# ScalarE takes the last sequence's last values and gates ahead of the first sequence's second normalisation

## The chip, the core and the metric

The kernel runs on one NeuronCore of a Trainium2 chip. The time is device microseconds of one launch, from the first to the last work of the core; the median of several runs is compared. A profiled execution of the kernel gives the span (first to last instruction) and the trace.

## What is computed

A decoder layer for four sequences of 1024 tokens with 256 features, in three stages, each followed by a layer normalisation of input plus result:

```python
# stage 1: gated convolution and a linear recurrence
proj = einsum('btd,ed->bte', x, W_in)          # gate and value halves
g = sigmoid(gate); v = conv5(val) + conv_b     # depthwise, 5 taps
h = tanh(a_param) * h + g * v                  # scan over the tokens
y1 = layernorm(x + einsum('btd,ed->bte', h, W_out)) * ln_w + ln_b
x = layernorm(x + y1)                          # "second normalisation"
# stage 2: three iterations of attention from 1024 slots on 64 context rows, each with a GRU cell
x = layernorm(x + slots)
# stage 3: every token goes to the expert (of 8) with the highest score
x = layernorm(x + (x + expert(x)))
```

## The kernel before

The first stage runs sequence by sequence (b = 0 to 3), in two chunks of 128 features (c = 0, 1), all within the first 170 us. Each engine has one hand-written list of steps, which it works through strictly in the order of the code; semaphores tie the lists together. What happens around the change:

- TensorE, `project(b)` (line 1152) makes the values and gates in PSUM, two banks each; `output(b)` (line 1167) multiplies the scanned result by W_out, in two halves of four token tiles; `transposes(b)` (line 1188) turns the normalised rows feature-major; `low_parts(b)` (line 1197) subtract the rounded part from what was turned. Its list reads: `project(3, 1, C)`, `transposes(0)`, `output(2, 0, TJ)`, `low_parts(0)`, `output(2, TJ, NT)`, `transposes(1)`, `spread(0)`, `low_parts(1)`, `first_scores(0)` (line 1267).
- ScalarE, `values(b, c)` (lines 551 to 569) copies the values out of PSUM, makes the first convolution tap with its bias, and the gates with a sigmoid; `window(w)` (line 571) loads the table with logarithm and exponential and makes reciprocal standard deviations; `first_rows` and `second_rows(b)` (lines 584 and 590) apply a normalisation to eight tiles of rows; `new_slots(b)` (line 651) copies the turned rows out of PSUM, twice; `row_roots` (line 596) and `low_slots` (line 662) follow.
- VectorE, `taps` (line 1632) makes the other four convolution taps, `scan` (line 1650) the recurrence, `residual(b)` (line 1661) adds `output(b)` to x in four pairs of tiles and takes the statistics, `second(b)` (lines 1703 to 1713) prepares the second normalisation, `offsets(w)` (lines 1680 to 1688) follows `window(w)`, and `first_tops` (line 1729) reads the first scores.
- GpSimd makes one product of gates and convolution per sequence (line 983) and adds a bias (line 976).

Three waits matter here. `transposes(0)` waits for all sixteen gate copies, which the last step of `values(3, 1)` completes, for the low value parts, and per tile for `n2_done`, which `second_rows(0)` counts up. `residual(2)` comes behind `offsets(2)` on VectorE, and the second half of `output(2)` needs a PSUM bank that the first pair of `residual(2)` frees. `rss[:, 1]`, which `second_rows(0)` reads as its scale, is written again by `window(2)`.

Of the kernel before, what the change touches and what calls it, by code (L numbers as in the profile page):

```python
# [27 lines left out]
def decoder_layer(nc, x, xT, ctxT, vecs, w_inT, w_outT, wq, wkT, wvT, wihT, whhT, gateT, expertT,  # L28
# [7 lines left out]
    NT = T // P  # L36
# [36 lines left out]
    with root:  # L73
# [5 lines left out]
        def sem(name):  # L79
            return root.enter_context(nc.semaphore(name))  # L80
# [27 lines left out]
        def col(c, i):  # L108
            return vec[:, c, i:i + 1]
# [37 lines left out]
        n1_done, n2_done = sem("n1_done"), sem("n2_done")  # L147
# [261 lines left out]
        def value_bank(i):  # L409
            return TBS[i % 2]  # L410

        def high_part(i):
            return 4 * (i // 2) + i % 2
# [4 lines left out]
        def cols_of(j):  # L418
            return slice(j * BANK, (j + 1) * BANK)
# [4 lines left out]
        with nc.Block(no_gpsimd_drain=True) as block:  # L424
# [125 lines left out]
            def _(act):  # L550
                def values(b, c):
                    n = C * b + c
                    if b > 0:
                        act.wait_ge(conv, TAPS * (n - C + 1))
                    for j in range(J):
                        act.wait_ge(val_mm, J * n + j + 1)
                        act.activation(val[:, c, HALO + j * BANK:HALO + (j + 1) * BANK],
                                       psum[:, VB + j, :], ACT.Copy).then_inc(val_ev, 1)
                    act.wait_ge(val_ev, J * n + J)
                    if b > 1:  # L560
                        act.wait_ge(scanned, n - 2 * C + 1)
                    act.activation(cvs[b % 2][:, c, :], val[:, c, 0:T], ACT.Identity, bias=col(c, V_CB),
                                   scale=col(c, 0)).then_inc(tap_act, 1)
                    if b > 1:
                        act.wait_ge(out_mm, NT * (b - 1))
                    for j in range(J):
                        act.wait_ge(gate_mm, J * n + j + 1)
                        act.activation(gates[:, b % 2, c, cols_of(j)], psum[:, GB + j, :],
                                       ACT.Sigmoid).then_inc(gate_ev, 1)

                def window(w):

                    lo, hi, n1, n2 = WINDOWS[w]
                    if w in (1, 2, 6):
                        act.preload_act_table_set("natural_log_exp_and_others")
                    if n1 > 0:
                        act.wait_ge(agg1, NT * n1)
                    if n2 > 0:
                        act.wait_ge(agg2, NT * n2)
                    act.activation(rss[:, lo:hi], mvs[:, lo:hi, :, 1], ACT.Ln, bias=epsc[:, 2:3]).then_inc(ln_act, 1)  # L580
                    act.wait_ge(ln_act, 2 * w + 1)
                    act.activation(rss[:, lo:hi], rss[:, lo:hi], ACT.Exp, scale=-0.5).then_inc(ln_act, 1)
# [7 lines left out]
                def second_rows(b, lo=0, hi=NT):  # L590
                    act.wait_ge(off2, b + 1)
                    for t in range(lo, hi):
                        act.activation(res[:, b % 2, t, :], res[:, b % 2, t, :], ACT.Identity,
                                       bias=nms[:, 1, t:t + 1], scale=rss[:, 1, t:t + 1]).then_inc(n2_done, 1)
# [40 lines left out]
                def free_part(n):  # L635
                    if n > 2:
                        act.wait_ge(vp_out[n % 3], 64 * (n // 3))
# [7 lines left out]
                def value_low(i):  # L645
                    act.wait_ge(vp_sub, i + 1)
                    free_part(high_part(i) + 2)
                    act.activation(value_parts[(high_part(i) + 2) % 3][:], psum[:, value_bank(i), 0:HG],
                                   ACT.Copy).then_inc(vp_lo, 1)
# [62 lines left out]
                values(3, 0)  # L712
                value_low(2)
                value_low(3)
                second_rows(0)
                values(3, 1)
                window(2)
                new_slots(0)
                row_roots(1)
# [1654 lines left out]
```

## Time and profile before

| what | value |
|---|---|
| median of 3 runs | 556.05 us (555.78 to 556.29) |
| profiled execution | 555.52 us |
| its span | 553.7 us |
| mean granted clock of TensorE | 0.963 |
| busy in the span: TensorE, VectorE, ScalarE, GpSimd | 91%, 79%, 61%, 45% |

The profiled execution's time is 1.8 us longer than its span, for what lies around the first and the last instruction. In the rows below PE is TensorE, PEld its weight loads, DVE is VectorE, ACT ScalarE and POOL GpSimd. "128x512 f32<-128x512 f32" is the shape written and read. Matmuls are pipelined, so one started while another still runs.

### The profile page before, as it was taken

How to read it: one execution, taken by the hardware profiler on the slowest of the kernel's cores; microseconds unless marked ns; L12 is line 12 of the kernel's file. 1: busy time of each engine (PE TensorE's matmuls, PEld its weight loads, DVE VectorE, ACT ScalarE, POOL GpSimd, SP SyncE). 2: the span in 40 equal slices, each digit the busy share in tenths (PEclk: the TensorE clock that was granted, in tenths of full speed). 3: DMA queues.
4: the chain of work that ended last, by engine and by line, in shares of the span. 5: the costliest groups of instructions: out<-in, count | busy, mean ns of one | idle time of the engine just before them, and what ended most of it. 6: DMA issues, size and time to landing. Idle time of an engine off the chain costs nothing.

```text
span 553.7 us, 7262 instructions
## 1 busy us (share of the span) xinstructions
PE 504.1 (91%) x2154; PEld 363.6 (66%) x2154; DVE 440.0 (79%) x794; ACT 340.5 (61%) x600; POOL 251.7 (45%) x217
## 2 busy tenths in 40 slices
PE   6999986959779999899999999999997999979992
PEld 2465552725557687488768867885885788767771
DVE  2999999998799487989967985897677567868882
ACT  4557539784697574667466656765663766557452
POOL 0123050400223256556835664575335156737776
PEclk9999999879889999999999999999997999989997
DMA  8950435420021031000000000002111136255742
GB/s 286 336 189 2 124 67 140 125 78 1 0 77 72 6 78 77 0 2 0 2 0 1 0 0 1 1 2 76 40 38 38 39 126 237 87 163 161 235 138 71
DMA packets 30661, 43.13 MB, mean 78 GB/s; under 512 B 7933, under 2 KB 22398, under 8 KB 30336
## 3 DMA queue, kind: packets, MB, share of 16 engines
q1 hardware_dynamic: 27216, 34.25, 20.5%
q0 software_dynamic: 3408, 8.43, 4.2%
q8 instruction: 18, 0.29, 0.2%
q14 instruction: 19, 0.16, 0.1%
HBM read 25.70 MB, written 16.83 MB: 77 GB/s over the span
## 4 chain that ended last, share of the span: by engine, by line
PE 51%; issue 6%; DVE 6%; POOL 4%; ACT 3%; DMA 1%; SPq 0%; POOLq 0%; ACTq 0%; DVEq 0%
PE psum L1456 35%; PE psum L1549 7%; PE psum L1267 3%; PE psum L1398 2%; PE psum L1520 2%; PE psum L1344 1%; POOL gru L1019 1%; DVE gru L1872 1%; POOL out L1057 1%; POOL sorted_rows L1049 1%; DVE slots_full L1874 1%; POOL slots_lo L1034 1%; PE psum L1356 1%; DVE gru L1852 1%; PE psum L1420 1%
## 5 line engine op out<-in xcount | busy, mean ns | idle before, releaser
L1456 PE MATMUL psum<-slots_hi,w_hh 128*128 128x512 f32 x560 | 181.5, 406 | 1.2 <-ACT gru L766 1.2
L1456 PEld LDWEIGHTS psum<-slots_hi,w_hh 128*128 128x128 f32 x560 | 104.5, 191 | 27.9 <-issue 4.2
L1019 POOL TENSOR_TENSOR gru<-slots_full,gru 128x512 f32<-128x512 f32 x43 | 65.9, 1531 | 111.6 <-ACT gru L772 111.6
L1456 PE MATMUL psum<-slots_lo,w_hh 128*128 128x512 f32 x280 | 112.3, 401 | 0.0
L1456 PE MATMUL psum<-at,v_ih_pair 128*128 128x512 f32 x288 | 92.6, 406 | 4.6 <-DVE at L1751 3.1
L772 ACT ACTIVATE gru<-gru,vec 128x512 f32<-128x512 f32 x48 | 34.7, 722 | 59.1 <-DVE gru L1852 59.0
L1456 PEld LDWEIGHTS psum<-at,v_ih_pair 128*128 128x128 f32 x288 | 54.6, 193 | 21.6 <-DVE at L1751 3.4
L1845 DVE SCALAR_TENSOR_TENSOR gru<-psum,vec,gru 128x512 f32<-128x512 f32 x48 | 35.9, 748 | 35.6 <-PE psum L1456 29.8
L1152 PE MATMUL psum<-early_hi,w_in 128*128 128x512 f32 x128 | 57.3, 606 | 5.2 <-DMA early_hi<-in_xT 5.1
L1456 PEld LDWEIGHTS psum<-slots_lo,w_hh 128*128 128x128 f32 x280 | 53.4, 191 | 12.9
L1872 DVE TENSOR_TENSOR gru<-gru 128x512 f32<-128x512 f32 x47 | 43.7, 930 | 7.2 <-POOL gru L1019 3.7
L1152 PEld LDWEIGHTS psum<-early_hi,w_in 128*128 128x128 f32 x128 | 24.6, 195 | 35.5 <-issue 33.9
L1034 POOL TENSOR_TENSOR slots_lo<-slots_full,slots_hi 128x512 fp32r<-128x512 f32 x32 | 47.1, 1473 | 0.6 <-DVE slots_hi L1898 0.6
L766 ACT ACTIVATE gru<-psum,brz 128x512 f32<-128x512 f32 x48 | 32.7, 681 | 21.4 <-PE psum L1456 21.3
L1874 DVE TENSOR_TENSOR slots_full<-gru 128x512 f32<-128x512 f32 x47 | 44.5, 947 | 1.6
L1549 PE MATMUL psum<-slots_full,w_tile 128*128 x156 | 43.5, 401 | 0.4 <-issue 0.2
L1057 POOL DMA_INDIRECT out<-out_tile,out_index x39 | 38.0, 975 | 11.9 <-issue 8.5
L1049 POOL DMA_INDIRECT sorted_rows<-row_block,dest x32 | 33.8, 1056 | 19.9 <-DVE dest L1960 8.5
L1028 POOL TENSOR_TENSOR ss_block<-sq_block 128x512 f32<-128x512 f32 x16 | 22.3, 1396 | 40.3 <-ACT sq_block L787 36.8
L1852 DVE TENSOR_TENSOR gru<-psum,gru 128x512 f32<-128x512 f32 x48 | 33.2, 691 | 6.7 <-PE psum L1456 5.0
L779 ACT ACTIVATE gru<-psum,brz 128x512 f32<-128x512 f32 x48 | 32.6, 678 | 0.9 <-PE psum L1456 0.6
L1167 PE MATMUL psum<-w_out,gates 128*128 128x256 f32 x128 | 29.2, 382 | 4.2 <-DVE res L1661 3.5
(249 smaller groups left out, 868.1 us busy)
## 6 DMA issues: line engine op xcount, KB each, us to landing
gathered<-sorted_rows SPq DMA_DIRECT2D x39, 129.0 KB, 2.4
x_scratch<-slots_full SPq DMA_DIRECT2D x8, 512.0 KB, 3.0
x_block<-x_scratch SPq DMA_DIRECT2D x8, 512.0 KB, 4.3
early_hi<-in_xT SPq DMA_DIRECT2D x3, 1024.0 KB, 5.7
v_ih_pair<-value_part SPq DMA_DIRECT2D x32, 96.0 KB, 2.2
x_tm<-in_x SPq DMA_DIRECT2D x4, 512.0 KB, 7.0
slots_full<-expert_plus SPq DMA_DIRECT2D x1, 2048.0 KB, 10.1
sorted_rows<-gru SPq DMA_DIRECT2D x1, 1032.0 KB, 11.4
```

Of the source, the lines that this page charges most:

```text
L772: act.activation(X(u), X(u), ACT.Tanh, bias=col(c, V_BIH + 2)).then_inc(n_act, 1)
L1019: pool.tensor_tensor(DF(u), full[:, c, seq(k, h), blk(j)], X(u), ALU.subtract).then_inc(d_pool, 1)
L1034: last = pool.tensor_tensor(slots[1][:, c, b, blk(j)], full[:, c, b, blk(j)], slots[0][:, c, b, blk(j)].bitcast(F32), ALU.subtract)
L1049: pool.indirect_dma_start(rows[:], bass.IndirectOffsetOnAxis(dest[:, n:n + 1], 0), rowb[:, row_slot(n), :], None, bounds_check=E * REGION - 1,
L1057: pool.indirect_dma_start(out[:], bass.IndirectOffsetOnAxis(oidx[:, g % 4, t:t + 1], 0), og[:, i % (4 * TG), :], None, bounds_check=TOK - ...
L1152: last = pe.matmul(psum[:, bank + j, :], wi[:, k, at_col:at_col + P], xF[b % 2][:, k, cols_of(j)], start=k == 0, stop=k == C - 1)
L1456: last = pe.matmul(psum[:, bank, :], w, d, start=start and i == 0, stop=stop and i == len(pairs) - 1, skip_group_check=begun or late)
L1549: last = pe.matmul(expert_out(i), wT[:, i % TG, c, :], ew[:, c, bass.ds(off, D)], start=c == 0, stop=c == C - 1)
L1845: dve.scalar_tensor_tensor(out=X(u), in0=psum[:, hn_bank(u), :], scalar=col(c, V_BHH + 2), in1=X(u), op0=ALU.add, op1=ALU.mult).then_inc(t ...
L1852: dve.tensor_tensor(X(u), psum[:, XN_B, :], X(u), ALU.add).then_inc(t2_dve, 1)
L1872: dve.tensor_tensor(Z(u), Z(u), DF(u), ALU.mult).then_inc(e_dve, 1)
L1874: dve.tensor_tensor(full[:, c, seq(k, h), blk(j)], X(u), Z(u), ALU.add).then_inc(s_dve, 1)
```

## The change

ScalarE's list had `second_rows(0)` and then `values(3, 1)` behind the low value parts. Now `values(3, 1)` comes first. Since `second_rows(0)` then stands directly ahead of `window(2)`, which overwrites the scales that it reads, ScalarE waits between the two until all eight rows have been finished (`n2_done` at NT = 8).

```diff
                 values(3, 0)
                 value_low(2)
                 value_low(3)
+                values(3, 1)
                 second_rows(0)
-                values(3, 1)
+                act.wait_ge(n2_done, NT)
                 window(2)
                 new_slots(0)
                 row_roots(1)
```

No other engine's list is changed, and no instruction but the wait is added.

## Rows read from the trace of the kernel before

**Rows 1.** The page: busy us (share of the span) and instructions of each engine.

```profile
PE 504.1 (91%) x2154; PEld 363.6 (66%) x2154; DVE 440.0 (79%) x794; ACT 340.5 (61%) x600; POOL 251.7 (45%) x217
```

**Rows 2.** Timeline of ScalarE: start us, us, line, operation, tiles, count [idle before].

```profile
89.58 4.04 ACT L593 ACTIVATE res<-res,nms,rss 128x256 f32<-128x256 f32 x8
93.52 1.07 ACT L557 ACTIVATE early_lo<-psum 128x512 f32<-128x512 f32 x2
...
95.77 1.06 ACT L568 ACTIVATE gates<-psum 128x512 f32<-128x512 f32 x2
96.85 1.28 ACT L575 ACT_TABLE_LOAD   x1
...
98.59 0.58 ACT L659 ACTIVATE slots_full<-psum 128x512 f32<-128x512 f32 x1
...
101.93 0.66 ACT L660 ACTIVATE slots_hi<-psum 128x512 fp32r<-128x512 f32 x1
105.37 0.30 ACT L599 ACTIVATE rrs<-rrs,epsc 128x8 f32<-128x8 f32 x1 [2.78 <-DVE rrs L1688]
```

**Rows 3.** Timeline of TensorE, the last projection.

```profile
84.94 7.28 PE L1152 MATMUL psum<-early_hi,w_in 128*128 128x512 f32 x16
```

**Rows 4.** Timeline of TensorE, behind the last projection to the last transposes.

```profile
96.88 3.47 PE L1188 MATMUL psum<-ident,res 128*128 128x128 f32 x16 [4.66 <-ACT gates L568]
100.19 3.62 PE L1167 MATMUL psum<-w_out,gates 128*128 128x256 f32 x16
103.46 1.29 PE L1197 MATMUL psum<-slots_hi,neg 128*128 128x512 f32 x4
106.08 3.69 PE L1167 MATMUL psum<-w_out,gates 128*128 128x256 f32 x16 [1.33 <-DVE res L1661]
...
123.18 5.70 PE L1267 MATMUL psum<-slots_full,fold 128*64 128x512 f32 x16 [1.19 <-ACT slots_lo L667]
...
148.62 1.22 PE L1456 MATMUL psum<-at,v_ih_pair 128*128 128x512 f32 x2 [3.13 <-DVE at L1751]
...
162.76 0.73 PE L1456 MATMUL psum<-at,v_ih_pair 128*128 128x512 f32 x2 [1.42 <-DVE gru L1852]
165.03 2.17 PE L1188 MATMUL psum<-ident,res 128*128 128x128 f32 x8 [1.54 <-ACT res L593]
```

**Rows 5.** Timeline of VectorE, from the last taps to the first scores.

```profile
97.37 5.43 DVE L1632 SCALAR_TENSOR_TENSOR slots_full<-early_lo,vec,slots_full 128x1024 f32<-128x1024 f32 x4
...
102.99 2.35 DVE L1688 TENSOR_TENSOR rrs<-rrs,rss 128x8 f32<-128x8 f32 x1
105.25 0.68 DVE L1661 TENSOR_TENSOR res<-psum,x_tm 128x512 f32<-128x512 f32 x1
...
109.81 0.69 DVE L1661 TENSOR_TENSOR res<-psum,x_tm 128x512 f32<-128x512 f32 x1 [0.25 <-PE psum L1167]
...
129.02 1.23 DVE L1729 CUSTOM_DVE_ANT_0 sc<-psum,inv 128x1024 f32<-128x1024 f32 x1 [0.77 <-PE psum L1267]
```

**Rows 6.** Stretches: length, each engine's busy time (count), granted clock, DMA share, GB/s.

```profile
96.00:98.00 2.00, 1.12 (x5) 1.12 (x6) 2.00 (x2) 1.98 (x3) 0.00 (x0) 0.65 1.10 314
100.00:102.00 2.00, 2.00 (x12) 1.79 (x11) 1.79 (x3) 2.00 (x6) 0.00 (x0) 0.99 0.28 108
...
104.00:106.00 2.00, 0.75 (x4) 0.27 (x2) 1.97 (x3) 0.60 (x3) 1.31 (x1) 1.00 0.36 133
...
148.00:152.00 4.00, 3.38 (x8) 2.74 (x9) 3.04 (x4) 3.43 (x8) 0.00 (x0) 0.50 0.00 0
...
164.00:168.00 4.00, 2.97 (x11) 2.17 (x12) 3.87 (x5) 4.00 (x9) 2.38 (x6) 0.61 0.00 0
```

**Rows 7.** The chain that ended last, in order of time: start us, us, what.

```profile
228.49 3.65 PE psum L1267 x16
...
424.12 1.25 PE psum L1398 x4
...
427.89 0.47 PE psum L1398 x4
```

## The prediction

> **What bounds the kernel now.** I read the page first. TensorE is busy for 91% of the span and VectorE for 79% [rows 1]. A share over the whole span says nothing of one stage, so I went to the stretch that the diff touches, 84 to 130 us, one engine at a time, and asked of each engine where it stood idle and for whom.
>
> ScalarE runs without a gap from the eight rows of `second_rows(0)` (89.58) through `values(3, 1)` (93.52 to 96.83), the table load (96.85) and `window(2)` to the last piece of `new_slots(0)` (101.93 to 102.59). Then it stands for 2.78 us, until VectorE has written `rrs` [rows 2]. So ScalarE's finish in this stage has slack.
>
> TensorE ends `project(3, 1, C)` at 84.94 + 7.28 = 92.22 [rows 3] and stands 4.66 us for the gates of `values(3, 1)`, because `transposes(0)` waits for the last gate. Then come the transposes (96.88), the first half of `output(2)` (100.19), the low parts (103.46 to 104.75), another 1.33 us of waiting for VectorE's residual sum, and the second half of `output(2)` (106.08 to 109.77) [rows 4].
>
> VectorE is the one that doesn't stop: four convolution taps from 97.37, then `offsets(2)`, whose last instruction takes 2.35 us beside GpSimd's product of the same time, then the four residual pairs. Its only wait is 0.25 us ahead of the fourth pair, for the second half of `output(2)` [rows 5]. Both other engines meet VectorE here, ScalarE at 105.37 and TensorE at 106.08. VectorE sets the time, with TensorE's second half of `output(2)` 0.25 us behind it.
>
> **The change, part by part.** It adds no work but one wait, and moves two blocks past each other. *The block of ScalarE.* `values(3, 1)` took 96.83 - 93.52 = 3.31 us; put at 89.58 it ends at 92.89. Its inputs are there: its last gate half would start some 2.7 us into the block, about 92.3, and the matmul that feeds it ends at 92.22 [rows 2, 3]. The margin is under 0.1 us, so this wait costs nothing to 0.1 us. The eight rows take 4.04 us and overlap their neighbour by 0.1, so they end at about 96.8, where the old order ended. The table load starts there as before; no load is added, because the rows use a function that needed none at 89.58 either. The sum on ScalarE is 3.31 + 4.04 either way.
>
> *The added wait* (`n2_done` for all eight rows) stands behind the last row. The load of before starts 0.02 us after the end of the preceding instruction anyway, so I take 0 and bound it by 0.1 us, the overlap that back-to-back activations show. Queued behind it are the load, `window(2)`, `new_slots(0)` and `row_roots(1)`; those who want them are VectorE's `offsets(2)`, which stands behind the taps that end at 102.80 and so comes 4 us after the `window(2)` of before, and TensorE's low parts. The 2.78 us of idle time hide all of it. If that cover were gone, it would cost its 0.1 us.
>
> *Who gets what earlier or later.* The first convolution tap comes 3.9 us earlier, and VectorE wants it only behind `residual(2)`, whose fourth pair starts at 109.81 [rows 5]. The rows of `second_rows(0)` come 3.2 us later, and only the transposes read them. `transposes(0)` can now follow the rows one by one, from about 93.4 to 97.3 rather than 96.88 to 100.35. `new_slots(0)` found its transposes ready at 98.59 before, and is held by ScalarE's own order, so it gains nothing. The first half of `output(2)` starts when VectorE's scan ends, about 97.4 by the taps behind it [rows 5], rather than at 100.19, and ends near 101.1. VectorE reads it first at 105.25, so this gains nothing either. The DMA queue issues what it issued, at the same events. Some 3 us of TensorE's time are freed, but all of them are freed ahead of a rendezvous at 106.08 that VectorE sets. The gain is 0.
>
> *The price to look for* is TensorE's clock. The wait of 4.66 us goes. In its place, after the first half of `output(2)` ends near 101.1, there are only four low parts, tied to the pieces of `new_slots(0)` (the last ready at 102.6), and then nothing from about 103.0 to 106.08: 3.0 us idle where there were 1.33. The trace shows what gaps do. It fell to half, 1.2 GHz, in the gap of 4.66 us, at about 96.6 (0.65 over 96 to 98), ahead of 148.62 after 3.13 us idle (0.50 over 148 to 152), and ahead of 165.03, where 0.73 us of matmul stood between gaps of 1.42 and 1.54 us. It did not fall in the 1.33 us ahead of 106.08 [rows 4, 6]. The new gap with its sparse forerun is nearest to that of 148.62, so I hold a fall near 106 to 107 for likelier than not, 7 in 10. Its cost: the first cold stretch lasted from 96.6 to 100.0, 3.4 us (0.99 over 100 to 102) [rows 6]. Half the matmuls of a warm stretch of that length are lost, so the second half of `output(2)` ends some 1.7 us later (3.69 us for 16 warm; all cold, 7.4 us, is the upper end, 3.7 us more). VectorE's fourth pair already waits, so that passes straight on to the statistics, to `window(3)` and to `first_rows(2)`.
>
> From there it can grow or shrink. It grows to about 2.5 us if the first scores, 5.70 us in the trace for 16 matmuls that take 3.65 when warm [rows 4, 7], then run wholly cold (7.3 us, 1.6 more, less the 0.8 us that VectorE waits for them at 129.02 [rows 5]). It shrinks where a later cold stretch on the chain moves or goes: that of 164 to 168 (0.61, so 3.1 of 4 us at half [rows 6]) holds the last transposes and costs about 1.6 us now, and the chain at 424.12 shows 1.25 us for four matmuls that take 0.47 at 427.89 [rows 7]. So the cost of a fall, carried to the end, lies between -1 and +2.5 us.
>
> A rule of the Trainium skill ("TensorE: Matmul & The Clock Gate", Part 1) is that the array drops to half rate after being idle long enough and warms again only after sustained work, and that the monitor runs free of the kernel's own start, so that the place of the drop can vary between runs. By that rule the fall is to be feared here. The trace agrees with both levels; the runs of before, within 0.5 us of each other, don't show the variation.
>
> **The rivals.** *A, forecast: no change that can be measured.* Either the clock doesn't fall in the new gap (3 in 10; the gap is split by four low parts, or the late transposes still bring the old fall and the first half of `output(2)` runs cold and fills the gap), or it falls and later stretches give most of it back. For it: every edge that the change moves ends at VectorE's queue. Change 0 to +0.7 us. Sum: 555.52 (the profiled execution) + 0.1 = 555.62; the median of the runs lies 0.53 above that execution, so 556.15.
>
> *B, slower: the clock falls ahead of the second half of `output(2)`* and the 1.7 to 2.5 us stay. It decides from the point where TensorE ends those 16 matmuls more than 0.25 us after VectorE wants them, and is over the bound from 1.1 us on. Against it: the two give-backs. Time 557.7 to 558.6.
>
> *C, faster.* Either a shifted cold stretch at 165 or 421 is lost by the shift and nothing is paid for it, which is worth 1.6 us less what the first fall cost, or the freed 3 us reach someone whom I hold to be covered. Time about 554.5 to 554.9. *D: the change does not do what it says*, because the last gate half waits for TensorE: then `transposes(0)` starts up to 0.1 us later. It ends in A, as the 2.78 us hide it.
>
> **How the numbers follow.** A measurement of this kernel can tell about 0.2%, 1.1 us, from no change. A (with D) 0.55, B 0.33, C 0.12. The forecast is A's 556.15. The range reaches from inside C, 554.8, to B's end, 558.6; outside are about half of C and a little of B. Faster 0.12, same 0.55, slower 0.33.
>
> **What would show it.** In the changed profile: `values(3, 1)` at about 89.6 and the rows of `second_rows(0)` at 92.8 with no gap; transposes from 93.4 at the pace of the rows; the table load at 96.8 to 96.95; TensorE idle from about 103 to 106.1; ScalarE idle again ahead of `rrs` at 105.37. The granted clock from 106 to 110 decides between A and B: if it is full, the fourth residual pair starts at 109.8; if it is at half, at about 111.4. Wrong would be a residual pair that starts before 105.25, or a ScalarE that reaches 102.6 much later.

## The result

The changed kernel took 557.68 us in the median of 6 runs (557.37 to 559.64), beside 555.91 us for the kernel before in the median of 6 (554.89 to 557.00): 1.77 us more, a ratio of 1.004 with a 95% interval of 1.0023 to 1.0056. By the ratio the change makes this kernel slower by 0.4%, and the interval does not contain 1. The profiled execution took 559.64 us, the slowest of its six, with a span of 557.8 us. So the trace shows the loss larger than the median does: its span is 4.1 us longer than that of before, where the medians differ by 1.77.

The page of the changed kernel, busy time, and the granted clock in 40 slices:

```profile
PE 506.5 (91%) x2154; PEld 362.9 (65%) x2154; DVE 439.4 (79%) x794; ACT 340.6 (61%) x600; POOL 251.4 (45%) x217
...
PEclk9999999777998999999999999999998999989997
```

Instruction counts are those of [rows 1], and VectorE and ScalarE are busy for as long as before within 0.6 us. What was added is not work. TensorE's 2.4 us more of busy time is the same matmuls taking longer. Over the whole span its mean granted clock is no lower than before (0.964 and 0.963), so the average hides the cause: what counts is which matmuls run in the cold stretches (those at half clock).

**ScalarE, where the change was made.** The changed kernel's timeline of ScalarE:

```profile
89.85 1.12 ACT L557 ACTIVATE early_lo<-psum 128x512 f32<-128x512 f32 x2
...
92.14 1.06 ACT L568 ACTIVATE gates<-psum 128x512 f32<-128x512 f32 x2
93.10 4.04 ACT L593 ACTIVATE res<-res,nms,rss 128x256 f32<-128x256 f32 x8
97.16 1.28 ACT L575 ACT_TABLE_LOAD   x1
...
102.25 0.66 ACT L660 ACTIVATE slots_hi<-psum 128x512 fp32r<-128x512 f32 x1
105.61 0.30 ACT L599 ACTIVATE rrs<-rrs,epsc 128x8 f32<-128x8 f32 x1 [2.71 <-DVE rrs L1689]
```

This execution was 0.26 us later than that of before from well ahead of the change (its last projection starts at 85.20, that of [rows 3] at 84.94). Taken off, the last piece of `new_slots(0)` starts at 101.99, where it stood at 101.93 in [rows 2]. The swap and the added wait together cost ScalarE 0.06 us, and the idle time behind hides it: 2.71 us where there were 2.78. The side that was edited loses nothing.

**TensorE, where the loss is.** Its timeline in the changed kernel (compare [rows 4]):

```profile
93.84 3.79 PE L1189 MATMUL psum<-ident,res 128*128 128x128 f32 x16 [1.36 <-ACT res L593]
97.79 3.72 PE L1168 MATMUL psum<-w_out,gates 128*128 128x256 f32 x16 [0.16 <-DVE gates L1651]
101.16 1.31 PE L1198 MATMUL psum<-slots_hi,neg 128*128 128x512 f32 x3
102.95 0.49 PE L1198 MATMUL psum<-slots_hi,neg 128*128 128x512 f32 x1 [0.48 <-ACT slots_hi L660]
106.33 6.27 PE L1168 MATMUL psum<-w_out,gates 128*128 128x256 f32 x16 [2.88 <-DVE res L1662]
...
126.01 6.62 PE L1268 MATMUL psum<-slots_full,fold 128*64 128x512 f32 x16 [1.19 <-ACT slots_lo L667]
```

The transposes follow the rows from 93.84 and the first half of `output(2)` starts as soon as VectorE's scan is done, so the 4.66 us of idle time are gone. But the second half still starts when VectorE frees its bank, at 106.33. The idle time has moved there: 2.88 us where there were 1.33. Then the same 16 matmuls take 6.27 us instead of 3.69. The stretches of the changed kernel say why (length, busy time of the five engines, granted clock, DMA share, GB/s; compare [rows 6]):

```profile
96.00:98.00 2.00, 1.68 (x9) 0.82 (x8) 2.00 (x2) 1.98 (x4) 0.00 (x0) 1.00 1.09 324
...
102.00:104.00 2.00, 0.97 (x2) 0.35 (x2) 1.97 (x4) 0.90 (x2) 0.78 (x1) 1.00 0.75 284
104.00:106.00 2.00, 0.00 (x0) 0.00 (x0) 2.00 (x2) 0.35 (x2) 1.56 (x1) 0.68 0.51 193
106.00:108.00 2.00, 1.67 (x4) 1.43 (x5) 1.93 (x6) 2.00 (x6) 1.63 (x2) 0.50 0.00 0
...
110.00:112.00 2.00, 2.00 (x8) 1.60 (x6) 1.45 (x3) 2.00 (x5) 1.11 (x1) 0.61 0.00 0
```

The granted clock fell to half (1.2 GHz) in the new gap, at about 104.7, and came back between 110 and 112. The half clock lasted 6.8 us. In the kernel before it fell at about 96.6 and was full again from 100 on, after 3.4 us. The cold stretch has moved from work that nobody waited for (the transposes) to work that VectorE waits for, as VectorE's timeline shows:

```profile
105.50 0.68 DVE L1662 TENSOR_TENSOR res<-psum,x_tm 128x512 f32<-128x512 f32 x1
...
110.11 0.69 DVE L1662 TENSOR_TENSOR res<-psum,x_tm 128x512 f32<-128x512 f32 x1 [1.77 <-PE psum L1168]
...
112.63 0.69 DVE L1662 TENSOR_TENSOR res<-psum,x_tm 128x512 f32<-128x512 f32 x1 [1.04 <-PE psum L1168]
...
132.78 1.23 DVE L1730 CUSTOM_DVE_ANT_0 sc<-psum,inv 128x1024 f32<-128x1024 f32 x1 [1.70 <-PE psum L1268]
```

VectorE now waits 1.77 + 1.04 us where it waited 0.25 [rows 5], so the fourth pair is late by 112.63 - 109.81 - 0.26 = 2.56 us, which is the sum of the waits less the 0.25. At the first scores the delay is 132.78 - 129.02 - 0.26 = 3.50 us, because those ran cold almost to their end: they took 0.92 us more (6.62 us for 5.70), and VectorE's wait for them grew by 0.93 (1.70 for 0.77). After that it changes little: the scores of the first full round of units start at 232.65 in the chain of waits against 228.49 in [rows 7], 3.9 us later with the offset taken off, and the spans differ by 4.1 us.

### The profile page after: what moved, and what is told of

Its sections match the earlier page's. It is cut to its first block, busy times and chain, and to the rows that moved or that the text cites. A ratio compares the mean times of both kernels' runs of the same rounds, so it can differ in the third digit from the quotient of the medians.

```text
span 557.8 us, 7262 instructions
## 1 busy us (share of the span) xinstructions
PE 506.5 (91%) x2154; PEld 362.9 (65%) x2154; DVE 439.4 (79%) x794; ACT 340.6 (61%) x600; POOL 251.4 (45%) x217
## 4 chain that ended last, share of the span: by engine, by line
PE 51%; issue 6%; DVE 6%; POOL 4%; ACT 3%; DMA 1%; SPq 0%; POOLq 0%; ACTq 0%; DVEq 0%
PE psum L1457 35%; PE psum L1550 7%; PE psum L1268 3%; PE psum L1399 2%; PE psum L1521 2%; PE psum L1345 1%; POOL gru L1020 1%; DVE gru L1873 1%; POOL sorted_rows L1050 1%; POOL out L1058 1%; DVE slots_full L1875 1%; POOL slots_lo L1035 1%; PE psum L1357 1%; PE psum L1421 1%; DVE gru L1853 1%
## 5 line engine op out<-in xcount | busy, mean ns | idle before, releaser
L1457 PE MATMUL psum<-at,v_ih_pair 128*128 128x512 f32 x288 | 91.1, 400 | 5.1 <-DVE at L1752 3.1
L1168 PE MATMUL psum<-w_out,gates 128*128 128x256 f32 x128 | 31.8, 407 | 5.3 <-DVE res L1662 4.5
```

The source lines that it names most:

```text
L1457: last = pe.matmul(psum[:, bank, :], w, d, start=start and i == 0, stop=stop and i == len(pairs) - 1, skip_group_check=begun or late)
```

## Experiments

The two theories: *the clock* (the moved idle time lets TensorE's clock fall just ahead of matmuls that VectorE waits for), and *ScalarE's side* (the new order or its added wait costs the time in a way that the profile hides). In each session the kernel before ran on the same chip; its median was 555.90, 555.95 and 556.82 us.

**The changed kernel again.**

> The changed kernel again, for a yardstick on this chip beside the others. Both theories: 1.3 to 2.5 us above the kernel before, about 557.7. In the profile the second half of output(2) (16 matmuls behind the gap of 2.9 us) takes 5 to 6.5 us at half clock, where the kernel before took 3.69.

558.07 us (557.12 to 558.75, 7 runs) against 555.90 (554.61 to 557.92, 30 runs), ratio 1.0041 (1.0024 to 1.0059). TensorE's timeline in its trace, and two stretches of it:

```profile
98.10 4.15 PE L1168 MATMUL psum<-w_out,gates 128*128 128x256 f32 x16
...
106.64 6.67 PE L1168 MATMUL psum<-w_out,gates 128*128 128x256 f32 x16 [2.87 <-DVE res L1662]
```

```profile
94.00:96.00 2.00, 1.73 (x8) 0.88 (x8) 1.97 (x3) 2.00 (x6) 0.00 (x0) 0.90 0.98 321
...
104.00:106.00 2.00, 0.00 (x0) 0.00 (x0) 2.00 (x2) 0.07 (x1) 1.87 (x1) 0.96 0.68 255
```

The time is as expected, and the trace is a second sample of the mechanism; the 6.67 us lie just above the 5 to 6.5 expected. The clock fell twice here, at about 95.6 and, after it had been full again from 99, at about 105.8. So the earlier fall didn't prevent the second one: the first half of `output(2)` ran partly cold (4.15 us for 3.72), and a gap of 2.87 us was still left.

**Fill the gap.** The change stays as it is; TensorE gets work to do in the gap.

```diff
+                def keep_busy(n, bank=2):
+
+                    for _ in range(n):
+                        pe.matmul(psum[:, bank, 0:D], ident[:], wo[:, 0, :], start=True, stop=True)
+
...
                 low_parts(0)
+                keep_busy(6)
                 output(2, TJ, NT)
```

> The changed kernel with six extra f32 matmuls (twelve instructions as traced, 2.7 us at full clock) on TensorE between low_parts(0) and the second half of output(2), into a bank that nobody reads; their result is not used. Clock theory: the gap shrinks from 2.9 to about 0.2 us, the granted clock stays full from 104 to 112, the second half of output(2) takes 3.7 us again, VectorE's fourth pair waits 0.2 to 0.3 us, and the time is back within 0.5 us of the kernel before. Rival theory (ScalarE's new order or its added wait costs the time, and the clock is a bystander): the time stays 1.3 to 2.5 us above the kernel before, or more by the extra work.

556.00 us (12 runs), ratio to the kernel before 1.0007 (0.9995 to 1.0019). The median lies 0.1 us above that of the kernel before, so the loss is gone, with more work on the engine than either kernel has. TensorE's timeline and, in the last line, VectorE's fourth pair:

```profile
104.09 2.75 PE L1305 MATMUL psum<-w_out,ident 128*128 128x256 f32 x12
107.13 3.69 PE L1168 MATMUL psum<-w_out,gates 128*128 128x256 f32 x16 [0.29 <-DVE res L1668]
```

```profile
110.86 0.69 DVE L1668 TENSOR_TENSOR res<-psum,x_tm 128x512 f32<-128x512 f32 x1 [0.25 <-PE psum L1168]
```

The second half is back at 3.69 us and VectorE's wait at 0.25, to the digit those of before. ScalarE's order and its wait are those of the change. The rival theory expected 1.3 us or more; the interval ends at 0.19%, 1.1 us.

**Fill a third of the gap.** As above with `keep_busy(2)`.

> As the last, with two extra matmuls (0.9 us at full clock), so that about 2.0 us of the gap stay. Clock theory: somewhere between; a gap of 2.1 us ahead of a residual step at 71 us left the clock full in the kernel before, so I expect no fall in most executions and a time 0 to 1.2 us above the kernel before. Rival theory: 1.3 to 2.5 us above.

556.29 us (554.97 to 558.81, 12 runs), ratio 1.0008 (0.9991 to 1.0025). In the median it lies in the expected band, but in the profiled execution (558.31 us) the clock fell in the gap of 2.0 us:

```profile
106.83 5.19 PE L1168 MATMUL psum<-w_out,gates 128*128 128x256 f32 x16 [2.01 <-DVE res L1668]
```

with a granted clock of 0.61 over 106 to 108. The gap of 2.12 us at 71 us in the kernel before, where the clock stayed full, was no safe bound. Two of the twelve runs (558.31 and 558.81) lie above all 30 of the kernel before (up to 557.92), and seven lie at 556.33 or below. I read it as falling in some executions and not in others; one trace doesn't show that, nor in how many.

**Hold the transposes back.** ScalarE keeps the new order, TensorE gets its old block back.

```diff
                         pe.wait_ge(fold_ev, C)
                         pe.wait_ge(vp_lo, B)
+                        pe.wait_ge(n2_done, NT)
```

> The changed kernel with one more wait on TensorE: transposes(0) starts only when all eight rows of second_rows(0) are done. ScalarE keeps the new order and its added wait, and TensorE gets back the block of before (transposes from about 97.2, first half of output(2) to about 104, low parts to about 105, gap ahead of the second half about 1.2 us). Clock theory: time within 0.3 us of the kernel before. Rival theory (ScalarE's side): 1.3 to 2.5 us above it.

555.93 us (12 runs), ratio 1.0012 (0.9997 to 1.0026). TensorE's timeline:

```profile
97.70 3.65 PE L1190 MATMUL psum<-ident,res 128*128 128x128 f32 x16 [4.90 <-ACT res L593]
101.14 4.36 PE L1168 MATMUL psum<-w_out,gates 128*128 128x256 f32 x16
105.15 1.28 PE L1199 MATMUL psum<-slots_hi,neg 128*128 128x512 f32 x4
106.66 3.69 PE L1168 MATMUL psum<-w_out,gates 128*128 128x256 f32 x16 [0.23 <-DVE res L1663]
```

Making TensorE wait longer takes the loss away: the median is that of the kernel before within 0.03 us. The block is late and partly cold (4.36 us for the first half), but it is not waited for, and it closes the gap in front of the half that is, to 0.23 us, where I had expected about 1.2. By the interval a cost of up to 0.26% (1.4 us) for ScalarE's side can't be excluded from these runs alone; those of the full filling leave 1.1, and in the traces ScalarE was late by 0.06 us and nobody waited for it.

**The gap without the change.** The kernel before, with ScalarE untouched, and the first half of `output(2)` cut down to one matmul of 64 columns per tile instead of two of 256. This leaves out part of the output projection for four tiles of the third sequence.

```diff
+                        if b == 2 and t < TJ:
+                            last = pe.matmul(psum[:, OB + q % 2, (t % 2) * D:(t % 2) * D + 64],
+                                             gates[:, b % 2, 0, t * P:(t + 1) * P], wo[:, 0, 0:64],
+                                             start=True, stop=True)
+                            last.then_inc(out_mm, 1)
+                            continue
```

> The kernel before, ScalarE's order untouched, but the first half of output(2) shrunk to eight traced matmul instructions of 64 columns (of the four tiles' 16 of 256), so that its result is cut short there; it ends near 101.2 instead of 103.8. The gap ahead of the second half of output(2) then is about 3.0 us as in the changed kernel. Clock theory: the granted clock falls in that gap in most executions, the second half takes 5 to 6.5 us, and the time is 1 to 2 us above the kernel before although there is less work. Rival theory (ScalarE's side of the change costs the time): no change, 555.9.

558.08 us (557.39 to 560.01, 6 runs) against 555.95 (24 runs), ratio 1.0051 (1.0032 to 1.0071). TensorE:

```profile
99.61 1.64 PE L1167 MATMUL psum<-w_out,gates 128*128 128x64 f32 x8
101.06 1.01 PE L1203 MATMUL psum<-slots_hi,neg 128*128 128x512 f32 x3
102.55 0.50 PE L1203 MATMUL psum<-slots_hi,neg 128*128 128x512 f32 x1 [0.48 <-ACT slots_hi L660]
105.96 6.26 PE L1173 MATMUL psum<-w_out,gates 128*128 128x256 f32 x16 [2.92 <-DVE res L1667]
```

VectorE's third and fourth pairs:

```profile
109.75 0.69 DVE L1667 TENSOR_TENSOR res<-psum,x_tm 128x512 f32<-128x512 f32 x1 [1.77 <-PE psum L1173]
...
112.27 0.69 DVE L1667 TENSOR_TENSOR res<-psum,x_tm 128x512 f32<-128x512 f32 x1 [1.04 <-PE psum L1173]
```

Less work for TensorE, and 2.1 us more by the medians, as with the change. The gap of 2.92 us is near the changed kernel's 2.88, the duration behind it is 6.26 us for 6.27, and VectorE's two waits are the same to the digit. The clock theory is shown from both sides: filling the gap takes the loss away, and opening it without the change brings it.

**What other cold stretches cost.** The prediction had counted on later cold stretches moving or going. Three kernels take them away from the kernel before by small matmuls of `ident` on itself into an idle bank, at the places named in the expectations, for example:

```diff
                 spread(0, OB)
+                keep_busy(16)
                 low_parts(1)
```

> The kernel before with extra small matmuls on TensorE (results unused, an idle bank) in the gap of 4.1 us ahead of low_parts(1) and between those. Clock theory: the first scores run warm, 3.7 us instead of 5.0 to 6.6, VectorE no longer waits for them (0.8 us in the trace of before), time 0.5 to 1 us below the kernel before. Rival theory (the extra matmuls get in the way): 0 to 1 us above.

554.97 us (12 runs), ratio 0.9983 (0.9967 to 0.9999). As expected. The first scores and VectorE's reading of them:

```profile
123.42 3.65 PE L1269 MATMUL psum<-slots_full,fold 128*64 128x512 f32 x16 [0.59 <-ACT slots_lo L667]
```

```profile
128.46 1.23 DVE L1738 CUSTOM_DVE_ANT_0 sc<-psum,inv 128x1024 f32<-128x1024 f32 x1
```

They are warm (at full clock), 3.65 us, and VectorE no longer waits for them. The interval ends just below 1.

> The kernel before with extra small matmuls only in the two gaps of 1.4 and 1.5 us ahead of the last transposes (about 161.3 to 165.0). Clock theory: the last transposes and the unit behind them run warm; where the clock fell there, which it does in some executions only, 1.6 us are saved, so 0.3 to 1.6 us below the kernel before in the median. Rival theory: no change, as another engine has slack to give, or up to 0.5 us above.

554.52 us (12 runs), ratio 0.9983 (0.9968 to 0.9997). The last transposes run at full clock:

```profile
164.00:168.00 4.00, 3.63 (x24) 2.60 (x24) 3.87 (x5) 4.00 (x8) 2.40 (x6) 1.00 0.00 0
```

where [rows 6] had 0.61 over the same stretch. By the ratio it is worth about 0.9 us, by the medians 1.4, both in the expected band.

> The kernel before with the fillers of the last two, and also in the gaps of 2.3 and 0.7 us ahead of the token tiles at 417 to 424 and in the gap of 2.4 us ahead of the first gathered tile at 487. Clock theory: no cold stretch between 104 and the last tiles; 0.8 + 1.6 + 1.7 + 1.6 us if each were cold in every execution, 1.5 to 4 us below the kernel before in the median, and a narrower spread of its runs than the 3.3 us of before. Rival theory: no change or up to 1 us above.

553.39 us (552.15 to 555.27, 7 runs), ratio 0.9959 (0.9941 to 0.9978): 2.6 us by the medians. The spread of its runs is 3.1 us, no narrower than the 3.0 us of the 24 runs beside it, so that part of the expectation was wrong. So was the one of no cold stretch behind 104: in its trace they stood at 134 to 138 and 151 to 155, where nothing had been filled.

**Both together.** Does the time that the change frees on TensorE become worth something once the clock is looked after?

> The changed kernel with all the fillers of the earlier run on the kernel before (ahead of the low parts of sequence 1, the last transposes, the token tiles, the first gathered tile) and twelve more small matmuls (2.7 us) in the gap that the change opens, behind low_parts(0). Clock theory, with the finding that the 3 us which the change frees reach nobody: the same time as the kernel before with those fillers, within 0.4 us, so 2 to 3 us below the kernel before. Rival (the freed 3 us are worth something once the clock stays full): 1 us or more below that kernel.

> The kernel before with all the fillers once more, beside the last on the same chip: about 553.4, ratio 0.996 to the kernel before.

On one chip, where the kernel before took 556.82 us (19 runs): the changed kernel with all fillers 553.23 us (8 runs), ratio 0.9944 (0.9922 to 0.9965); the kernel before with the fillers 554.11 us (12 runs), ratio 0.9962 (0.9946 to 0.9977). The medians lie 0.9 us apart, which misses the expected 0.4, but the intervals overlap, so whether the change is worth anything then is open. The second came out at the expected ratio. In the trace of the first, the granted clock fell only once ahead of the last tiles, over 96 to 100. Its gap behind `low_parts(0)`:

```profile
104.16 2.84 PE L1307 MATMUL psum<-ident 128*128 128x128 f32 x24
107.21 3.69 PE L1168 MATMUL psum<-w_out,gates 128*128 128x256 f32 x16 [0.21 <-DVE res L1689]
```

By these ratios both are faster than the kernel before, and so than the changed kernel.

## Why the prediction was half right

The forecast was A, no change that can be measured, at 556.15 us. What came was B, the rival that had a third of the chance. The time lies in the range and next to B's 557.7, but the likeliest case was the wrong one. That it came within 0.1 us of B's figure is partly luck: B counted 1.7 us at the fourth pair, and the two traces show 2.6 and 3.0 there.

*ScalarE's block* held: no gap, no added table load, 0.06 us for the swap and the wait where 0 to 0.1 stood. Rival D (the last gate half waits for TensorE) did not happen: the gates start at 92.14 and end without an extra wait.

*Who gets what earlier* held in each item. The transposes followed the rows (93.84), the first half of `output(2)` started at 97.79, and nobody used either. The gain was 0, as worked out.

*The fall of the clock* held: forecast near 106 to 107 with 7 in 10, seen at about 104.7 in the changed kernel's trace and at about 105.8 in the second one, so inside the gap rather than at its end. The trace of the kernel with the gap and no change has it too. One of the reasons for no fall, that the old fall might come first and the first half of `output(2)` run cold and fill the gap, failed in the second trace: the old fall came, and the gap was 2.87 us.

*Its size* was too small. The term was 1.7 us at the fourth pair, from a cold stretch of 3.4 us as in the trace of before. The cold stretch lasted from 104.7 to about 111.5, and so the matmuls from 106.33 were cold nearly to their end: 2.58 us more for the 16, 2.56 us at the fourth pair. In the second trace VectorE waited 1.77 and 1.43 us. The estimate took the length of one cold stretch for the length of all. The trace of before had a longer one in view: by the granted clock of its stretches (0.50 over 148 to 152 in [rows 6], 0.67 over 152 to 156) the one at 148.62 lasted 6.8 us.

*What grows it* held as a place, but its sum was wrong. The forecast took the 0.8 us that VectorE waits for the first scores off their growth. A wait that is already there is no cover; every microsecond that the scores take longer is added to it. In the first trace they took 0.92 us more and the wait grew by 0.93, which took the delay to 3.5 us, above the upper end of 2.5. In the second they took 0.57 us less (5.13 us), the wait fell to 0.20, and that gave back 0.6 us.

*The give-back is the step that failed.* The forecast A leaned on "later stretches give most of it back" wherever the clock fell. The traces show what became of the later stretches. Stretches as in [rows 6], the granted clock third from the end; of the kernel before, of the changed kernel, and of its second trace:

```profile
420.00:424.00 4.00, 3.41 (x12) 2.21 (x11) 3.51 (x4) 0.50 (x2) 2.83 (x2) 0.61 0.00 0
488.00:492.00 4.00, 2.68 (x12) 2.69 (x13) 0.64 (x4) 0.86 (x2) 2.23 (x3) 0.64 0.68 189
```

```profile
168.00:172.00 4.00, 3.12 (x11) 2.18 (x12) 3.90 (x4) 4.00 (x9) 2.15 (x6) 0.70 0.00 0
492.00:496.00 4.00, 2.58 (x13) 2.59 (x14) 0.76 (x5) 1.03 (x3) 2.11 (x3) 0.73 0.72 188
```

```profile
168.00:172.00 4.00, 4.00 (x13) 3.00 (x14) 3.90 (x5) 4.00 (x9) 1.35 (x6) 0.50 0.00 0
420.00:424.00 4.00, 1.69 (x8) 1.02 (x7) 3.87 (x6) 1.20 (x2) 1.94 (x1) 1.00 0.00 0
488.00:492.00 4.00, 2.14 (x20) 2.03 (x18) 3.40 (x13) 2.25 (x4) 0.00 (x0) 1.00 0.39 115
```

In the first execution nothing was given back: the last transposes start at 168.80, again at half clock, in 2.17 us as before, and the clock fell again at the late tiles, near 429 and 494. In the second the clock stayed full at 421 and 489, where that of before had fallen, which gave back some 2.7 us, but it stayed at half over 167 to 174, where before it had been 3.4 us, which cost 1.3. With the offset of 0.6 us taken off, this execution was late by 2.4 us at the last transposes (168.00), by 3.7 at the scores of the first full round (232.75), by 1.0 at 494.64, and by 1.8 at its end (spans of 556.1 and 553.7).

What I had read as fixed features of the kernel before, which a delay might dodge, are draws: each execution has its own set, the kernel before as well, by the mean granted clocks of its runs (0.963 to 0.976). The 30 runs of the kernel before beside the second trace spread over 3.3 us. The 11 of them with a mean granted clock of 0.975 or more have a median of 555.04 us, the other 19 one of 556.30. The changed kernel has the same two kinds of runs, and both are later: 557.12 us for the one run at 0.976, 558.22 in the median of the other six. A delay doesn't escape the draws on average. Of the 2.6 to 3.0 us at the fourth pair the medians of the two sessions keep 1.8 and 2.2, so most of the loss stays, where A had most of it given back. Two traces don't show how the rest splits between executions in which the clock stays full and luckier stretches behind. The three runs of the kernel before that the prediction had agreed within 0.5 us by chance, and I took that agreement for evidence that the cold stretches stay in place.

The rule cited ahead, of the Trainium skill's page "TensorE: Matmul & The Clock Gate", Part 1, says that the monitor runs free of the kernel's start; there I held the runs of before against it. The traces of these sessions agree with the page. The first fall came at about 95.6 in the second trace of the changed kernel and at 104.7 in the first, with the same code ahead of both.

Weighed rightly, the fall at 7 in 10 and no expected give-back would have made B the forecast, at 557.7.

## What to carry to other kernels

Before taking idle time from TensorE, ask where it goes: if the next rendezvous is set by another engine, the gap only moves, and it may move from ahead of work that nobody waits for to ahead of work on the chain, which then runs at half clock. In these traces the clock fell in gaps of 2.0 and 2.9 us, stayed full in others of 1.3 and 2.1, and fell where gaps of 1.4 and 1.5 us stood close together (ahead of 165.03), so the length of a single gap doesn't tell. A few matmuls into an idle bank filled such gaps at no cost that the runs can show (ratio 1.0007), took all of this loss away, and took 2.6 us by the medians off the kernel before (0.9959). When a forecast leans on cold stretches of one trace, treat their places as draws, while a delay ahead of them stays on average. And a wait that is already there doesn't absorb a growth of the work waited for; it passes it on.

## What the runs showed that I had not expected

A gap of 2.01 us let the clock fall in one trace (5.19 us for 16 matmuls behind it), where the kernel before had 1.33 us in front of the same matmuls, and 2.12 us at 71 us, and no fall. A cold stretch can last 3.4 us (96.6 to 100.0 before) or 6.8 us (104.7 to 111.5 after). The place of the first fall differed between executions of one kernel by some 9 us, and the spread of the kernel before's runs was 3.3 us in 30 runs on one chip, six times that of the three runs ahead of the prediction. Work that is cold is not lost when it isn't waited for: the held transposes and the first half behind them took up to 4.36 us, and the kernel's median was 0.03 us from that of before.
